# Moving three of the four 128-column comparisons of each count unit from VectorE to GpSimd

## The reference, cut to what matters

```python
def gcn_conv(x, edge_index, W, b):
    n = x.shape[0]
    loop = jnp.arange(n)
    src = jnp.concatenate([edge_index[0], loop])
    dst = jnp.concatenate([edge_index[1], loop])
    xw = x @ W.T
    deg = jax.ops.segment_sum(jnp.ones_like(dst, dtype=x.dtype), dst, num_segments=n)
    dinv = jnp.where(deg > 0, jax.lax.rsqrt(deg), 0.0)
    norm = dinv[src] * dinv[dst]
    msg = xw[src] * norm[:, None]
    out = jax.ops.segment_sum(msg, dst, num_segments=n)
    return out + b
h = jax.nn.relu(gcn_conv(x, edge_index, W1, b1))
h = jax.nn.relu(gcn_conv(h, edge_index, W2, b2))
```

## Time and profile before

| | |
|---|---|
| median of 3 runs | 4388.67 us (4383.09 to 4389.2) |
| profiled execution | its span, first to last instruction: 5825.1 us; its time outside the span is not shown |
| PE, DVE, ACT, POOL busy | 3173.4, 3165.7, 2409.4, 2312.0 us |
| building of the counts | about 138 to 773 us of the span |
| its VectorE comparisons | 1176 of 128 columns at 251 ns, 1568 of 400 columns at 320 ns |
| GpSimd between 138 and 773 us | no instruction |

### The profile page before, as it was taken

The page is one execution under the profiler, slowest core; times in us unless marked ns, Lnnn a source line. Parts: engine busy times, 40 slices in busy tenths (PEclk is TensorE's granted clock), DMA queues, the critical chain, the costliest instruction groups (busy, mean ns, idle before and its releaser), DMA issues. The chain is left out here.

```text
span 5825.1 us, 61632 instructions
## 1 busy us (share of the span) xinstructions
PE 3173.4 (54%) x16208; PEld 1958.6 (34%) x16208; DVE 3165.7 (54%) x10115; ACT 2409.4 (41%) x5229; POOL 2312.0 (40%) x2409
## 2 busy tenths in 40 slices
PE   2888787623555555562155554555523555564563
PEld 1333343312333333342033333333311333343342
DVE  5999853513454554576064464555822455454466
ACT  0766630023444444443143443444433444444453
POOL 3000002074555455415545545544064545545422
PEclk7999998856777677786577777777756777777786
DMA  2111124221212222111112212211021212212110
GB/s 75 60 60 60 60 85 168 99 62 36 48 46 48 47 47 50 42 28 37 42 45 48 52 44 48 50 46 44 4 55 37 47 47 47 50 45 47 45 25 23
DMA packets 127624, 298.46 MB, mean 51 GB/s; under 512 B 45412, under 2 KB 74972, under 8 KB 123712
## 3 DMA queue, kind: packets, MB, share of 16 engines
q0 software_dynamic: 74976, 155.58, 11.6%
q1 hardware_dynamic: 52320, 139.24, 7.1%
HBM read 241.28 MB, written 53.38 MB: 51 GB/s over the span
## 5 line engine op out<-in xcount | busy, mean ns | idle before, releaser
L1400 POOL DMA_INDIRECT work<-table,lane_src x2184 | 2072.7, 949 | 1897.4 <-PE psum L1554 967.3
L1439 ACT ACTIVATE work<-work,middle_node_number 128x384 f16<-128x384 f16 x1587 | 958.0, 604 | 1997.8 <-DMA work<-table,lane_src 950.8
L1497 PE MATMUL psum<-work 128*128 128x396 bf16 (+1 forms) x5850 | 1360.1, 380 | 699.7 <-issue 464.9
L1554 PE MATMUL psum<-work 128*128 128x136 f32 x4836 | 827.7, 339 | 1004.9 <-DVE node_sums L1722 890.6
L1722 DVE TENSOR_TENSOR node_sums<-node_sums,psum 128x136 f32 x2418 | 561.3, 294 | 1455.8 <-remote 892.2
L1554 PEld LDWEIGHTS psum<-work 128*128 128x128 f32 x4836 | 778.8, 242 | 1085.0 <-issue 969.9
L1497 PEld LDWEIGHTS psum<-work 128*128 128x128 bf16 x5850 | 626.3, 109 | 1290.0 <-issue 758.1
L1442 ACT ACTIVATE work<-work 128x384 bf16<-128x384 f16 x1587 | 829.4, 523 | 50.4
L715 PE MATMUL psum<-work 128*128 128x448 f16 x2100 | 460.9, 358 | 47.4 <-issue 37.5
L744 DVE TENSOR_SCALAR work<-work 128x400 f16<-128x400 f16 x1568 | 468.3, 320 | 0.0
L772 PE MATMUL psum<-work 128*128 128x400 f16 x1568 | 342.1, 342 | 111.8 <-DVE work L744 90.9
(11 more groups left out here) (360 smaller groups left out, 2539.9 us busy)
## 6 DMA issues: line engine op xcount, KB each, us to landing
counts<-work SPq DMA_DIRECT2D x14, 2800.0 KB, 8.1
work<-counts SPq DMA_DIRECT2D x14, 2800.0 KB
work<-table,lane_src POOLq DMA_INDIRECT x2184
work<-spread SPq DMA_DIRECT2D x78, 256.0 KB
work<-masks SPq DMA_DIRECT2D x78, 128.0 KB
work<-source_rows SPq DMA_DIRECT2D x39, 192.0 KB
spread<-node_sums SPq DMA_DIRECT2D x4, 896.0 KB
table<-work SPq DMA_DIRECT2D x10, 330.0 KB
```

Of the source, the lines that this page charges most:

```text
L1400: pool.indirect_dma_start(m.ring[:, s % SLOTS, 0:F + H], None, m.d_table[H], bass.IndirectOffsetOnAxis(ap=m.src[:, s:s + 1], axis=0)).then ...
L1439: act.activation(away, rows_of(g, u), ACT.Abs, bias=m.low_tile[:, hi:hi + 1]).then_inc(far_known, 1)
L1497: mm = pe.matmul(aid_banks[:, k, 0:3 * (F + H)], hot_of(g, u)[:, k * P:(k + 1) * P], m.all_thirds[:, :, hi, 0:F + H], start=(hi == 0), sto ...
L1554: pe.matmul(sum_slot(s), m.onehot[b % 2][:, s % U, :], m.ring[:, s % SLOTS, :], start=True, stop=True).then_inc(product, 1)
```

## The change

GpSimd gets a program of its own in the building of the counts: for each unit it waits for the slot (`unit_done`), makes the three 128-column comparisons of tiles 0 to 2 and signals `lo_paired`. VectorE makes no 128-column comparison any more (with PAIRED = 3 the condition `PAIRED <= b < CB - 1` never holds). TensorE waits for `lo_paired` as well. CREGS goes from 14 to 28, so that a chunk has one register load of 28 numbers, and the row of these numbers moves in front of `count_row` in SBUF. The second convolution has the new load too. GpSimd's program is written out for all 392 units, without a loop.

```diff
-CREGS = 14
+CREGS = 28
+PAIRED = 3
     late = 4 * 8 * LANES + 8 * P + 9 * P
+    m.cj_row = m.arena[0:1, late:late + CG * P].bitcast(I32)
+    late += CG * P
     m.count_row = m.arena[:, late:late + EDGE_TILES]
     late += EDGE_TILES
-    m.cj_row = m.arena[0:1, late:late + CG * P].bitcast(I32)
-    late += CG * P
...
                     for b in range(CB):
-                        if b < CB - 1:
+                        if PAIRED <= b < CB - 1:
                             dve.tensor_scalar(m.hot_lo[:, d, b, :], m.iota_cols[:, 0:P], m.low[:, b, bass.ds(n, 1)], None, ALU.is_equal)
                         t = dve.tensor_scalar(m.hot_key[:, d, b, :], m.iota_cols[:], m.key[:, b, bass.ds(n, 1)], None, ALU.is_equal)
...
+        @block.gpsimd
+        def _(pool):
+            for n in range(CUNITS):
+                if n >= DEPTH:
+                    pool.wait_ge(unit_done, n - (DEPTH - 1))
+                for b in range(PAIRED):
+                    t = pool.tensor_scalar(m.hot_lo[:, n % DEPTH, b, :], m.iota_cols[:, 0:P], m.low[:, b, n:n + 1], None, ALU.is_equal)
+                t.then_inc(lo_paired, 1)
...
                     pe.wait_ge(hot, n + 1)
+                    pe.wait_ge(lo_paired, n + 1)
                     pe.wait_ge(lo_hot, n + 1)
```

More of the change, by code:

```diff
@@ L721, in build_counts_and_sum @@
 def build_counts_and_sum(nc, m):
-    ph, (hot, lo_away, lo_hot, unit_done, evacuated, stored0, stored1, produced, summed) = phase(
-        nc, "onehots_done", "last_low_distance", "last_low_onehot", "unit_counted", "unit_evacuated", "chunk_stored_0", "chunk_stored_1", "chunk_product", "unit_summed")
+    ph, (hot, lo_paired, lo_away, lo_hot, unit_done, evacuated, stored0, stored1, produced, summed) = phase(
+        nc, "onehots_done", "first_lows_onehot", "last_low_distance", "last_low_onehot", "unit_counted", "unit_evacuated", "chunk_stored_0", "chunk_stored_1", "chunk_product", "unit_summed")
     stored = (stored0, stored1)
```

## The result

The changed kernel takes 4450.46 us (median of 4, 4449.01 to 4452.48) against 4386.89 us before (median of 4, 4383.09 to 4389.2) in the same comparison. The ratio is 1.0146, 95% interval 1.0132 to 1.0161: 64 us slower, where 32 us faster was forecast.

The account below looks back on a forecast made before the run. VectorE was taken to bound the building at 1.50 us per unit; a pace of 1.38 gave -40 and -3 us, loads +11, together -32, so 4357 us from 4388.67. The range was 4275 to 4500.

Parts of the forecast that it names:

- VectorE bounds at 1.50 us, TensorE stands behind it at 1.24: Building of the counts: VectorE sets 1.50 us per unit; TensorE's 1.24 is the floor of any relief of VectorE.
- GpSimd's turn for 128 columns: Building: from release by VectorE to its own end, a GpSimd comparison takes 0.25 us, bounds 0.21 and 0.34.
- The head of an instruction lies under the other engine's turn: VectorE and GpSimd in SBUF: an instruction's first 0.13 to 0.14 us overlaps the other engine's turn.
- The exclusion: Building: GpSimd and VectorE take turns in SBUF, making a unit 1.38 us instead of TensorE's 1.24.
- The forecast sign: New profile: GpSimd's comparisons alone and those beside VectorE should differ by near 0.13 us.
- Register loads +16, net +11: Building: one load of 28 per chunk exposes 16 us over 12 chunks, 5 us won back, net 11 slower.
- The long-turn rival: Building: GpSimd's turn is 0.34 us, a unit 1.64, with loads 75 us slower, 4464; chance 0.18.
- The batch rival: Building: VectorE keeps the ports through four comparisons, then GpSimd does three; 1.87 us per unit, 165 us slower, 4554; chance 0.13.
- The chance of 0.33 for slower: Whole run: chance of being slower by more than 0.2% (9 us), against 0.55 for faster and 0.12 within.
- The time carries over in us from the long profile: Building lasts equally long in the 5825 us profile and the runs, so -32 us applies to 4388.67, giving 4357.

Follow-up runs that it names:

- half: Changed kernel with GpSimd's comparisons over 64 of the 128 columns, the other 64 left unwritten: 4283.29 us in one run.
- shadow: Changed kernel, but VectorE makes all comparisons and GpSimd repeats three per unit into unread slots, TensorE not waiting: 5993.37 us where the kernel before takes 5888.83.

## Why the prediction was wrong

- *VectorE bounds at 1.50 us, TensorE stands behind it at 1.24.* Right: as soon as GpSimd has less to do (two comparisons, or 64 columns) the building comes down to 553 us. A pace of 1.24 wasn't held in any run; the best that lasted were 1.31 (`half`), 1.34 with one comparison moved, and 1.29 and 1.49 in turn with two.
- *GpSimd's turn for 128 columns: "I take 0.25".* This is the step that failed. With its head of 0.13 it meant 0.38 us alone; measured are 0.593 at least by the records and 0.577 from start to start. The lower bound took its slope from a memset (0.81 ns a column), and I chose near to it because the data are contiguous. The slope of GpSimd's own TENSOR_SCALAR in the earlier trace rows was 2.0 ns; the measured one is 2.5 to 2.6. Even the upper end, 0.47 alone, was too low. The 0.26 us of 20 elements alone and 108 more at 2.0 ns are 0.48, at 2.6 ns 0.54 us.
- *The head of an instruction lies under the other engine's turn.* Right for the rows it came from, wrong as a discount on GpSimd's pace: when it is saturated and VectorE stands, its comparisons overlap by 0.02 us and not by 0.13, so three cost 1.73 us, and 1.79 to 1.90 beside VectorE. "Alone GpSimd needs 3 x 0.38 = 1.14 us" was the number to doubt.
- *The exclusion.* It exists, as argued from the earlier trace rows; it costs VectorE 0.13 us for each comparison of GpSimd in `shadow`. In the changed kernel VectorE has room for its share (1.28 us from its first comparison to behind the addition, against 1.79). GpSimd's share counts: of the 92 us that the building lost, about 46 are GpSimd's own pace (679 against 633 us) and about 46 its delay beside VectorE. The first half alone already makes the building longer; the second is read from the trace, where every comparison without VectorE beside it starts 0.577 us before the next, and no experiment isolates it. The forecast sign, a difference of 0.13 us between alone and beside, came out at 0.04 by the mean.
- *Register loads +16, net +11.* Wrong in sign. They bring 43 us by themselves. The trace had the hint: 1.31 and 3.17 us in strict alternation for the same number of words, which I took for a matter of the queue. In the changed kernel only the 21 to 24 us of the second convolution are seen, the rest hides behind GpSimd.
- *The long-turn rival* (4464, chance 0.18) had the right place and nearly the right time, but with a turn of 0.34 us and a pace of 1.64. The time agrees by luck: the pace was higher than it had, and the loads, which it had as a cost, were a gain. The batch rival's 1.87 us came nearest in pace; its mechanism isn't what the rows show, since VectorE waits for slots and GpSimd never waits. The chance of 0.33 for slower was too low for the same reason as the sum: no case priced a comparison on GpSimd, alone, above 0.47 us.
- *The time carries over in us from the long profile.* Right where both profiles are of the same speed: the difference of those spans is 67 us, of the runs 64. Against the first profile (5825.1 us) it can't be checked.

## What to carry to other kernels

Price a moved instruction by the engine's own rows of the same operation, with its slope, and never by another operation's slope; where the new engine ends up with three of them per step, the error counts three times. Read the pace from the starts: a record that got 67 ns shorter brought none. Then move only as much as balances: with the register part, worth 1% by itself, one or two of three comparisons gain 2.4%, and all three lose 1.5%. And count on the two engines delaying each other: with two moved, each had 1.15 us of work per unit and the pace was 1.39 (the mean of 1.29 and 1.49). And an edit that looks like bookkeeping, the place and length of a register load, was worth 43 us here, or minus 100 with its other half missing.

## What was not expected of the hardware

- A register load of VectorE's queue took 1.86 us for 28 words from an address on the 16-byte grid and 11.0 us from one 8 bytes off it while comparisons ran, 6.25 us in the second convolution. For 14 words it was 1.32 and 3.18. Why 28 words cost so much more than twice 14 stays open.
- GpSimd's comparison: from start to start 0.25 us and 2.6 ns a column, the same for float16 and float32 input, and no less with a constant operand.
- Who pays for the exclusion changed with the load: 0.23 us on GpSimd's one comparison beside a busy VectorE, 0.13 us on VectorE for each one of a full GpSimd.
- One chip ran the whole kernel in 5889 us and two others in 4387 and 4390, with equal times in the building of the counts. The cause is open.
- Behind the building, the first attention layer was 8 us shorter in the changed kernel (1009 against 1017 us), which is open too.
